# Attention block: score maxima with the queries on partitions, the shift in two halves, one rounding part on ScalarE

## The reference

```python
# x: 16 x 256 x 128 float32; 16 heads of 8
qkv = x @ attn_w.T + attn_b                 # per head: q, k, v of 8
scores = einsum('bhki,bhqi->bhkq', k, q) / sqrt(8)
scores = where(key <= query, scores, -10000)
probs = softmax(scores, over keys)
out = einsum('bhkq,bhkl->bhql', probs, v) -> 256 x 128, @ out_w.T + out_b
x = layernorm(x + out)
# int8 feed-forward: each row of x and each column of rhs scaled by its absolute maximum / 127,
# rounded, multiplied, scaled back
x = layernorm(x + ffn(x))
```

## Time and profile before

| | |
|---|---|
| median of 3 runs | 273.44 us (272.13 to 273.6) |
| the profiled execution | 273.3 us, its span 271.6 us |
| PE, DVE, ACT, POOL busy | 75%, 69%, 59%, 50% of the span |
| mean granted clock of PE | 0.952 |
| DMA | 32.82 MB, mean 121 GB/s |

### The profile page before, as it was taken

How to read it: one execution, slowest core, us unless ns; L and a number is a source line. 1 busy time by engine, 2 the same in 40 slices (tenths; PEclk the granted TensorE clock), 3 DMA queues, 4 the chain that set the end, 5 groups by cost and what they waited for, 6 DMA issues and landing times.

```text
span 271.6 us, 10973 instructions
## 1 busy us (share of the span) xinstructions
PE 203.1 (75%) x4398; PEld 133.9 (49%) x4399; DVE 186.8 (69%) x545; ACT 161.1 (59%) x349; POOL 135.2 (50%) x268
## 2 busy tenths in 40 slices
PE   7269758689886868686878787777778879799610
PEld 4156635456564545454646455545455556565300
DVE  3727834746786869696969696868789899644521
ACT  3811133644685858585767665666767668678420
POOL 7352303231617473737474746474746262445764
PEclk9999999957999999999999999999999999899955
DMA  4499391909283848647675849391929550110001
GB/s 135 160 188 226 68 216 28 230 25 183 94 148 132 139 158 124 175 105 192 104 193 102 196 80 220 66 231 35 242 52 212 108 93 6 42 36 10 19 21 39
DMA packets 50754, 32.82 MB, mean 121 GB/s; under 512 B 7184, under 2 KB 50704, under 8 KB 50704
## 3 DMA queue, kind: packets, MB, share of 16 engines
q1 hardware_dynamic: 50560, 31.93, 52.1%
q10 hardware_dynamic: 144, 0.20, 0.3%
HBM read 17.17 MB, written 14.68 MB: 117 GB/s over the span
## 4 chain that ended last, share of the span: by engine, by line
PE 29%; DMA 25%; DVE 20%; ACT 8%; SPq 7%; issue 7%; POOL 3%; POOLq 0%; ACTq 0%; DVEq 0%
DMA xt_in<-xt_dram 22%; DVE part_max L643 9%; PE act_bank L933 7%; PE pv_bank L910 7%; PE dve_bank L845 4%; ACT z L518 3%; PE act_bank L943 3%; SPq L330 2%; DVE key_max L652 2%; DVE ffn L749 2%; SPq L331 2%; ACT probs L470 2%; DMA k_stat<-imagek 2%; SPq L340 2%; DVE key_max L655 2%
## 5 line engine op out<-in xcount | busy, mean ns | idle before, releaser
L643 DVE TRANSPOSE_TENSOR_REDUCE part_max<-dve_bank 128x16 f32<-128x512 f32 x160 | 108.7, 702 | 31.3 <-PE dve_bank L856 29.4
L470 ACT ACTIVATE probs<-act_bank 128x512 f32<-128x512 f32 x160 | 88.3, 595 | 31.1 <-PE act_bank L856 30.3
L845 PE MATMUL dve_bank<-q_move,k_stat 48*64 48x256 bf16 (+3 forms) x1024 | 67.1, 251 | 2.0 <-DMA k_stat<-imagek 1.8
L845 PE MATMUL act_bank<-q_move,k_stat 50*64 50x256 bf16 (+3 forms) x1024 | 63.6, 242 | 0.0
L845 PEld LDWEIGHTS dve_bank<-q_move,k_stat 48*64 48x64 bf16 x1024 | 42.5, 115 | 22.5 <-issue 10.2
L910 PE MATMUL pv_bank<-probs,v_stat 128*32 128x256 f32 (+3 forms) x1024 | 50.6, 318 | 0.3 <-ACT probs L470 0.2
L856 PE MATMUL dve_bank<-causal,identb 64*64 64x256 bf16 (+1 forms) x320 | 44.4, 270 | 0.6 <-issue 0.6
L856 PE MATMUL act_bank<-causal,identb 64*64 64x256 bf16 (+1 forms) x320 | 42.3, 260 | 0.0
L422 POOL TENSOR_SCALAR rstd<-moments 128x2 f32<-128x2 f32 x32 | 7.4, 230 | 69.3 <-DVE moments L765 53.8
L845 PEld LDWEIGHTS act_bank<-q_move,k_stat 50*64 50x64 bf16 x1024 | 39.9, 111 | 1.6 <-issue 0.6
L933 PE MATMUL act_bank<-xt_in,wqkv 128*128 128x256 f32 x64 | 22.6, 490 | 14.7 <-DMA xt_in<-xt_dram 14.3
(11 more groups left out here) (87 smaller groups left out, 312.4 us busy)
## 6 DMA issues: line engine op xcount, KB each, us to landing
imageq<-qk_parts SPq DMA_DIRECT2D x32, 192.0 KB, 3.6
imagek<-qk_parts SPq DMA_DIRECT2D x32, 192.0 KB, 4.0
q_move<-imageq SPq DMA_DIRECT2D x32, 192.0 KB, 3.9
k_stat<-imagek SPq DMA_DIRECT2D x32, 192.0 KB, 4.5
xt_in<-xt_dram SPq DMA_DIRECT2D x16, 128.0 KB, 4.8
x_in<-x_dram SPq DMA_DIRECT2D x16, 128.0 KB, 3.5
out_dram<-o SPq DMA_DIRECT2D x16, 128.0 KB, 3.1
q_move<-shift SPq DMA_DIRECT2D x32, 8.0 KB
```

The source lines that it names most:

```text
L470: act.activation(probs[u][:, :], act_bank[at % ACT_BANKS][:, :], ACT.Exp, scale=SCALE).then_inc(act_emptied, 1)
L643: dve.tensor_reduce(out32, dve_bank[at % DVE_BANKS][:, :].rearrange("k (c q) -> k c q", q=32), op=ALU.max, axis=AX.X, apply_transpose=True ...
L845: pe.matmul(bank[64 * half:64 * half + 64, at:at + TOK - blk * KB], k_stat[slot][rows, head, blk * KB:(blk + 1) * KB], q_move[slot][rows, ...
```

## The change

- The maxima's matmuls have q as the weights and k as the moving data, so that a bank holds queries on partitions and keys along the free axis (`max_pieces`, `max_scores`). The reduction is a plain one along the free axis. A second mask, `causal_t`, serves the diagonal blocks.
- The maxima of a batch are joined, turned and made into the shift in two halves, for units 0 to 4 and 5 to 9. Half 0: join at step 0, turn and shift at step 3. Half 1: join at step 5, turn and shift at step 8. Each half of the shift is put into `q_move` by four transfers of 16 pieces of 128 bytes in place of two transfers of 128 pieces for the whole. Exponential units 0 and 5 each wait for their half.
- `project_v` and `v_from_psum` go from step 5 to step 8. In phase -1 `project_qk(3)` goes from step 3 to step 8.
- The middle part of q and k is made by ACT at step 9, after `round_z`, for batches 3 and later; before it DVE made it at step 8. DVE keeps batches 0 to 2.
- `xt_in` has six slots; four are loaded at the start, and a phase loads batch b + 6.

```diff
-QK_RING, XT_RING, RING = 4, 4, 3
+QK_RING, XT_RING, RING = 4, 6, 3
+XT_FIRST = 4
+def max_pieces(u):
+    kind, p0 = UNITS[u]
+    if kind == FULL:
+        return [(p0 + j, 3, TOK * j) for j in range(2)]
+    if kind == ENDS:
+        return [(p0 + j, blk, TOK * j + at) for j in range(2) for blk, at in ((2, KB), (0, 0))]
+    return [(p0 + j, 1, 2 * KB * j) for j in range(4)]
-ACT_EXTRAS = {1: [("zq", -3)], 3: [("q", 4), ("k", 4)], 5: [("v", 1)], 8: [("heads", -1)]}
-DVE_EXTRAS = {1: [("out", -2)], 3: [("ffn", -3)], 5: [("shift", 1)], 6: [("pv", -1)]}
+ACT_EXTRAS = {1: [("zq", -3)], 3: [("q", 4), ("k", 4)], 8: [("heads", -1), ("v", 1)]}
+DVE_EXTRAS = {1: [("out", -2)], 3: [("shift0", 1), ("ffn", -3)], 6: [("pv", -1)], 8: [("shift1", 1)]}
...
             def load_xt(b):
-                if not real(b) or b < XT_RING:
+                if not real(b) or b < XT_FIRST:
...
             def phase(b):
                 write_image(b + 3, 1)
+                load_shift(b + 1, 0)
                 load_x(b)
-                load_shift(b + 1)
+                if b < 0:
+                    load_shift(b + 1, 1)
                 read_image(b + 3)
-                load_xt(b + 5)
+                load_xt(b + 6)
                 write_image(b + 4, 0)
+                if b >= 0:
+                    load_shift(b + 1, 1)
                 store(b - 3)
...
+            def second_part(b):                      # ACT
+                if real(b):
+                    wait(act, qk_split, b, 2)
+                    act.activation(part[b % 2][1], qk_rest[:, :, :], ACT.Copy).then_inc(qk_split[1], 1)
...
-                dve.tensor_reduce(out32, dve_bank[at % DVE_BANKS][:, :].rearrange("k (c q) -> k c q", q=32),
-                                  op=ALU.max, axis=AX.X, apply_transpose=True).then_inc(dve_emptied, 1)
+                dve.tensor_reduce(top, keys, op=ALU.max, axis=AX.X).then_inc(dve_emptied, 1)
...
+            def join_maxima(b, s):
+                wait_place(dve, dve_emptied, DVE_AT, ("max", b, 5 * s + 4))
+                pairs = slice(4 * s, 4 * s + 4)
+                dve.tensor_reduce(query_max[:, pairs, 0:4:2], ends_max[:, pairs, :].rearrange("q p (n k) -> q p n k", n=2),
                                   op=ALU.max, axis=AX.X).then_inc(max_joined[1], 1)
...
+            def make_shift(b, s):
+                turned = dve_bank[at % DVE_BANKS][0:16, 0:128]
+                dve.tensor_scalar(shift[s][:, 0, :], turned, -1.0, None, ALU.mult).then_inc(shift_made[1], 1)
+                wait(dve, shift_made, b, s + 1)
+                dve.scalar_tensor_tensor(out=shift[s][:, 1, :], in0=turned, scalar=-1.0, in1=shift[s][:, 0, :],
+                                         op0=ALU.mult, op1=ALU.subtract).then_inc(dve_emptied, 1)
...
+            def turn_maxima(b, s):
+                wait(pe, max_joined, b, s + 1)
+                bank = dve_ring((f"shift{s}", b))
+                pe.matmul(bank[0:16, 0:128], query_max[:, 4 * s:4 * s + 4, :].rearrange("q p n -> q (p n)"), ident[:, :],
+                          start=True, stop=True).then_inc(dve_filled, 1)
```

More of the change, by code:

```diff
@@ L227, in build_program @@
         qk_loaded = [sem(f"qk_loaded{i}") for i in range(QK_RING)]
-        shift_loaded = sem("shift_loaded")
+        shift_loaded = [sem(f"shift_loaded{s}") for s in range(2)]
         stored = sem("stored")
@@ L380, in _ @@
             for half in range(2):
[L381 to L383 removed]
+                for m, sign in ((causal, 1), (causal_t, -1)):
+                    m = m[64 * half:64 * half + 64, :]
+                    step(pool.affine_select(out=m, in_=m, compare_op=ALU.is_gt, fill=0.0,
+                                            base=0, pattern=[[-sign, KB]], channel_multiplier=sign))
             assert done[0] == POOL_MASK, done[0]
@@ L646, in join_maxima @@
-            def join_maxima(b):
+                if kind == FULL:
+                    top = query_max[:, p0:p0 + 2, 3]
+                elif kind == ENDS:
+                    top = ends_max[:, p0:p0 + 2, 2:6]
+                else:
+                    top = query_max[:, p0:p0 + 4, 1]
+                if u == 0 or u == 5:
+                    wait_place(dve, dve_filled, DVE_AT, (f"shift{u // 5}", b - 1))
+                dve.wait_ge(dve_filled, at + 1)
+                keys = dve_bank[at % DVE_BANKS][:, :]
@@ L890, in scores @@
                     if for_exp:
-                        own = own_blocks(u, half, exp_bank)
+                        own = own_blocks(u, half, exp_bank, EXP_OWN[UNITS[u][0]], causal)
                         if half == 1:
@@ L913, in pv @@
                 last.then_inc(pv_done[1], 1)
-            def turn_maxima(b):
+            def turn_maxima(b, s):
                 if not real(b):
                     return
-                wait(pe, max_joined, b)
-                bank = dve_ring(("shift", b))
-                for s in range(2):
-                    for half in range(2):
-                        rows = slice(64 * s + 32 * half, 64 * s + 32 * half + 32)
-                        last = pe.matmul(bank[rows, 0:64], key_max[:, 32 * s:32 * s + 32], ident[:, 64 * half:64 * half + 64],
-                                         start=True, stop=True)
-                last.then_inc(dve_filled, 1)
+                wait(pe, max_joined, b, s + 1)
+                bank = dve_ring((f"shift{s}", b))
+                pe.matmul(bank[0:16, 0:128], query_max[:, 4 * s:4 * s + 4, :].rearrange("q p n -> q (p n)"), ident[:, :],
+                          start=True, stop=True).then_inc(dve_filled, 1)
             def project_qk(b, w):
@@ L1030, in phase @@
                         feed_forward(b - 3)
-                    if u == 5:
-                        turn_maxima(b + 1)
-                        project_v(b + 1)
                     if u == 6:
@@ L1039, in phase @@
                     if u == 8:
+                        turn_maxima(b + 1, 1)
+                        if b == -1:
+                            project_qk(b + 4, 0)
+                            project_qk(b + 4, 1)
                         turn_heads(b - 1)
+                        project_v(b + 1)
                         pv(b, 2)
```

116 lines of the change are left out of this document (55 added, 61 removed).

## The result

The changed kernel takes 264.63 us (median of 4 runs, 262.44 to 267.21) against 273.52 us (4 runs) on the same chips: the ratio is 0.9665, 95% interval 0.957 to 0.976. It is faster, but by 9 us, not by 30: outside the range of 236 to 256.

What follows compares the result with a forecast made beforehand. No engine was full; phases waited for the load of xt and the joined maxima. From the span of 271.6 us, start 1.7, eleven phases 27.6 and three phases 1.5 left 240.8, or 243 us as execution time; range 236 to 256.

Steps and rivals of the forecast that it cites:

- The wait for xt: At the projection of q and k: six slots remove 1.7 us of DVE and 0.9 of PE waits a phase.
- PE's clock, as I had left open: PE's granted clock was 0.67 from 53.65 to 69.08; if full afterwards, some early gain is the clock's.
- The join, the maxima, the shift on DVE: DVE's work a phase: joins 0.65 to 0.4 us, shift 0.59 to 1.12, ten maxima reductions 0.2 less.
- ACT's copy: Middle part moved to ACT: a 128x512 copy of 0.60 us, with 4.7 us of slack after POOL's copy.
- PE's wait for the joined maxima: At `turn_maxima`: 1.4 us a phase on PE goes, as each turn comes three steps after its join is queued.
- The period of 11.8: Steady phases fall from 14.3 to 11.8 us, DVE needing 10.9; 27.6 us over eleven phases.
- tail unchanged: After the eleven phases: three phases without q and k go from 11.9 to 11.4, 1.5 us; the end stays.
- the chain run through DVE: Sign of being right: in a steady stretch the chain runs through DVE, busy above 90% in steady phases.
- Rival D: Plain reductions cost more than transposing ones: gain gone from 0.90 us each, 280 us at 0.95; chance 0.04.
- I cost it at nothing, covered by these; uncovered, 3.1 us.: SP's six more shift transfers a phase, at about 0.52 us each, held covered by slack before their use.
- rival A's second half: A new wait takes half the gain, here because SP is late: period 12.9, 12 us more, 255; A's chance 0.22.
- The start: Before phase 0: first exponentials 1.2 us later at 34.6, but the projection near 36.2, not 37.94: 1.7 us gained.

Runs made afterwards that it cites:

- e4: The kernel before with only six slots for xt and the load of batch b + 6: 260.7 us, ratio 0.948.
- e1: The changed kernel with half 1 of the shift issued on SP before the first image half is written: 249.9 us, ratio 0.910.
- e7: The changed kernel, SP order kept, with two transfers for each half of the shift in place of four, 15 issues a phase for 19: 238.9 us, ratio 0.874.
- e10: e7 with the middle part of q and k back on DVE: 243.2 us, ratio 0.879.
- e6: e1 with two transfers for each half of the shift in place of four, 15 issues a phase for 19: 239.4 us, ratio 0.874.

## Why the prediction was wrong

**The wait for xt: right in kind, spread wrongly.** With six slots the wait is gone, and e4 shows it alone, 260.7 us, within the 255 to 262 that PE's and DVE's waits give. But my sum spread the gain over eleven equal phases of 14.3, and in e4 most of it lies in the first two, which took 15.7 and 15.4 us before. Part of that is PE's clock, as I had left open: the stretch at a granted clock of 0.67 has PE busy for 14.17 us, and in e4 phase 1 (45.81 to 57.51) has 10.25 at a clock of 1.00.

**The join, the maxima, the shift on DVE: right in size.** A join took 0.168 us (two, 0.34; I took 0.4), the shift's instructions 0.269 and 0.278 (I took 0.28), a plain reduction 0.685 (I took 0.68; the transposing one 0.702), ACT's copy 0.618 (I took 0.60). The estimates from the Trainium skill (VectorE: DVE Perf Modes, The TRN2 errata) were 0.66 and 0.61: the trace puts the first 4% and the second 1% higher. PE's wait for the joined maxima is gone.

**The period of 11.8: right for the engines; the 243 us in part by luck.** The best phases of e1 take 11.69, and e7, with no queue in the way, 11.92, with 11.8 from phase 0 to phase 11. The projections of q and k of e7's phases 1 and 11:

```profile
46.39 1.06 PE act_bank L974 x4
...
165.41 1.06 PE act_bank L974 x4
```

But e7's 238.9 us is 4 under the forecast, and the terms differ: before phase 0 it gained 2.7 (forecast 1.7), in the eleven phases 27.2 (27.6), after phase 11's start 5.2 (1.5, "tail unchanged"). Nor did the chain run through DVE, as I had said it should: in e7's page it is 45% PE and 25% DVE, PE is busy for 11.18 us of 11.92 and DVE for 10.81, and e10 shows that more work on DVE hardly lengthens the phase. Which coupling of the two sets the 11.92 stays open. Rival D fell: the reductions did not cost more.

**The step that failed: "I cost it at nothing, covered by these; uncovered, 3.1 us."** I compared each transfer of the shift with the step that needs it and found slack, and took the queue's load, 19 x 0.52, to be 10 of 12 us. Two things were wrong there. The price of an issue: 0.62, not 0.52, so 11.8 us a phase, all of the phase that I forecast. And the wait inside the queue: moving `second_part` from DVE's step 8 to ACT's step 9 moved the release of `write_image(b + 4, 0)`, which stands just before half 1 of the shift; I counted the move on ACT, DVE and POOL, and not on SP, though the code has the count of three. A queue that is worked in order has no slack of its own for one entry: issue time and waits add up over a phase, and where they pass the engines' period they become the period. That is rival A's second half ("or SP is late"), to which I gave 12 us; the changed kernel is 21.6 us over the forecast and 25.7 over e7.

**The clock.** The forecast had no term for PE's clock in the steady phases, which was full before. In the changed kernel it fell in some of the phases in which PE waited for the shift: PE stood from 104.12 to 106.21, worked again, and from 107 to some 110.5 its granted clock was at the lower of its two levels. The mean of such a phase is 0.89, and PE's work took 12.6 us there, for 11.1 at the full clock. How much of those 1.5 us lengthened the phase was not separated.

**The start: right, and 1.3 us better than forecast.** ACT makes the middle part of batch 3, then the first exponentials at 34.18 (forecast 34.6, before 33.36). The projection of q and k of batch 4 starts at 34.92 (forecast 36.2), not at 37.94, and ACT copies them out of PSUM from 36.10 on. ACT's timeline of the changed kernel:

```profile
33.52 0.63 ACT L508 ACTIVATE qk_parts<-qk_rest 128x512 bf16<-128x512 f32 x1 [1.14 <-POOL qk_parts L422]
34.18 2.06 ACT L491 ACTIVATE probs<-act_bank 128x512 f32<-128x512 f32 x4
36.10 0.86 ACT L503 ACTIVATE qk_f<-act_bank,bias 128x256 f32<-128x256 f32 x2
```

## What to carry to other kernels

Treat the issuing queue as an engine: sum its issues and its waits over one period and set them against the period you forecast, before asking whether a single transfer is early enough. When an instruction moves to another engine or a later step, look up every semaphore count that it feeds, also those of queues that have nothing else to do with it, and what stands behind these waits. A fix of the order was worth 15 us in the full queue (e1) and nothing once the queue had room (e6 and e7 are alike), and an entry is dear or free by what else the queue holds, so measure each in the kernel that it is meant for. And when a forecast spreads a gain over equal phases, look whether the phases are equal: here the first two held most of one.

## What the runs showed of the hardware

The duration of an issue on SP is not fixed. It averages 0.52 us in the kernel before, 0.62 in the changed one and 0.645 in e1, in the 80 us of the table. Single issues of large transfers last up to 1.2 us and more, as the second image transfer at 123.09 in e1 above, others of the same transfer 0.45. Four small shift transfers take 2.40 to 3.37 us, 0.60 to 0.84 each; before, two of the old form took 1.07. What makes some long was not tested.

A wait of PE for the shift, once in a phase, went with a fall of its granted clock in some phases and not in others. In the changed kernel between 83 and 197 us the waits of 2.09, 2.38, 2.72 and 1.86 us are in phases with a mean clock of 0.89, 0.89, 0.80 and 0.88, those of 1.32, 1.35 and 1.68 in phases with 1.00. In e1 a wait of 1.63 us has a mean clock of 0.88 and one of 1.72 has 1.00, so the length of the wait alone does not decide it.
